# A 4 KB transfer of negated row maxima, issued by GpSimd instead of ScalarE

## The reference

```python
x = x + tanh(g_xattn[0]) * xattn(layernorm(x), ctx)      # fp8-rounded product, per batch 512 x 512
h = layernorm(x)
fused = h @ (Wa * col_scale)                             # queries, keys, values
scores = einsum('bhtd,bhsd->bhts', Qf, Kf) / sqrt(32)
scores = where(causal, scores, lowest)
attn = softmax(scores, axis=-1)                          # exp(s - max of the row) / sum
out = einsum('bhts,bhsd->bhtd', attn, V)
x = x + tanh(g_ffn[0]) * (out @ Wp)
```

## Time and profile before

| | us |
|---|---|
| median of 3 runs (lowest, highest) | 531.11 (529.98, 533.79) |
| profiled execution | 531.24 |
| its span, first to last instruction | 529.5 |
| TensorE busy | 458.1 (87%), mean granted clock 0.959 |
| VectorE busy | 336.6 (64%) |
| ScalarE busy, issues of transfers not counted | 272.3 (51%) |
| GpSimd busy | 144.5 (27%) |

### The profile page before, as it was taken

One profiled execution on the slowest core, in us unless ns is written; L12 is line 12 of the kernel. 1 busy time (PEld: TensorE's weight loads), 2 busy tenths in 40 slices (PEclk: granted clock), 3 DMA queues, 4 the chain that ended last, 5 costly groups with the idle time before them and its releaser, 6 DMA issues.

```text
span 529.5 us, 7878 instructions
## 1 busy us (share of the span) xinstructions
PE 458.1 (87%) x2536; PEld 325.8 (62%) x2536; DVE 336.6 (64%) x1110; ACT 272.3 (51%) x530; POOL 144.5 (27%) x264
## 2 busy tenths in 40 slices
PE   0477777998889999998779999998898999999994
PEld 0355556765555788765554878865564878676762
DVE  4997442698995244598996242677997244556634
ACT  2994326695545461595636452495655324444430
POOL 5849161252215200243214300233122100111210
PEclk9999997999878999999987999998989999999999
DMA  6411434323500245314400244314400143333002
GB/s 232 165 34 48 158 85 105 81 49 96 145 2 2 71 105 159 95 35 101 138 19 2 51 104 136 125 26 99 98 6 2 45 102 93 82 95 106 22 20 80
DMA packets 28025, 42.62 MB, mean 80 GB/s; under 512 B 8272, under 2 KB 8528, under 8 KB 27984
## 3 DMA queue, kind: packets, MB, share of 16 engines
q1 hardware_dynamic: 26448, 41.97, 28.5%
q10 hardware_dynamic: 1536, 0.14, 0.2%
HBM read 12.59 MB, written 4.19 MB: 32 GB/s over the span
## 4 chain that ended last, share of the span: by engine, by line
PE 58%; ACT 18%; DVE 13%; SPq 3%; issue 3%; DMA 2%; POOL 2%; ACTq 1%; DVEq 0%; POOLq 0%
PE pv_bank L716 11%; PE mm_bank L564 7%; PE mm_bank L565 6%; PE mm_bank L566 6%; PE exp_bank L702 5%; DVE x_all L1201 5%; PE max_bank L685 5%; ACT work L984 4%; DVE max_bank L1235 3%; SPq L374 3%; PE mm_bank L743 2%; PE mm_bank L744 2%; PE mm_bank L745 2%; PE turn_bank L580 2%; ACT tile_buf L931 2%
## 5 line engine op out<-in xcount | busy, mean ns | idle before, releaser
L1235 DVE CUSTOM_DVE_ANT_0 max_bank<-max_bank,causal 128x512 f32<-128x512 f32 (+3 forms) x256 | 119.2, 517 | 65.4 <-PE max_bank L685 65.0
L482 POOL TENSOR_SCALAR_AFFINE_SELECT work<-work 128x384 f32<-128x384 f32 x64 | 33.4, 521 | 299.4 <-ACT work L984 299.4
L984 ACT ACTIVATE work<-exp_bank 128x512 f32<-128x512 f32 (+1 forms) x192 | 90.9, 526 | 25.5 <-PE exp_bank L702 24.5
L716 PE MATMUL pv_bank<-work,v_aug 128*33 128x256 f32 (+3 forms) x512 | 83.6, 473 | 0.0
L702 PE MATMUL exp_bank<-q_stack,k_stack 97*128 97x512 f32 (+3 forms) x256 | 68.9, 353 | 4.1 <-ACT work L984 1.6
L685 PE MATMUL max_bank<-k_stack,q_stack 96*128 96x512 f32 (+3 forms) x256 | 61.7, 342 | 10.4 <-DVE row_max L1235 6.5
L716 PEld LDWEIGHTS pv_bank<-work,v_aug 128*33 128x33 f32 x512 | 29.0, 118 | 54.2 <-issue 48.5
L1218 DVE SCALAR_TENSOR_TENSOR qk_lo<-mm_bank,col_root,qk_hi 128x512 fp32r<-128x512 f32 x32 | 24.0, 750 | 59.2 <-ACT qk_hi L957 59.1
L1201 DVE SCALAR_TENSOR_TENSOR x_all<-mm_bank,coef,x_all 128x128 f32<-128x128 f32 x224 | 61.0, 342 | 0.8 <-PE mm_bank L612 0.8
L685 PEld LDWEIGHTS max_bank<-k_stack,q_stack 96*128 96x128 f32 x256 | 45.9, 196 | 17.8 <-issue 7.0
L702 PEld LDWEIGHTS exp_bank<-q_stack,k_stack 97*128 97x128 f32 x256 | 43.3, 188 | 19.7 <-ACT work L984 9.0
(11 more groups left out here) (161 smaller groups left out, 812.6 us busy)
## 6 DMA issues: line engine op xcount, KB each, us to landing
q_stack<-qk_hi SPq DMA_DIRECT2D x128, 64.0 KB, 2.0
k_stack<-qk_hi SPq DMA_DIRECT2D x128, 64.0 KB, 2.0
x_all<-in_x SPq DMA_DIRECT2D x16, 256.0 KB, 4.0
ctx_raw<-in_ctx SPq DMA_DIRECT2D x16, 256.0 KB, 4.4
q_stack<-qk_lo SPq DMA_DIRECT2D x64, 64.0 KB, 2.0
k_stack<-qk_lo SPq DMA_DIRECT2D x64, 64.0 KB, 2.0
out<-x_all SPq DMA_DIRECT2D x16, 256.0 KB, 2.3
work<-in_L_ffn_Wa SPq DMA_DIRECT2D x3, 768.0 KB, 9.7
```

Source lines behind the costliest of these rows:

```text
L482: pool.affine_select(out=three, in_=three, compare_op=ALU.is_ge, fill=0.0, base=0, pattern=[[0, 3], [1, P]], channel_multiplier=-1)
L716: last = pe.matmul(pv_bank[64 * j:64 * j + D + 1, P * m:T], v_aug[:, m, 2 * u + j, :], prob[j][:, PROB_COL[m]:PROB_COL[m] + T - P * m], st ...
L984: act.activation(prob[j][:, UNIT_COL[k]:UNIT_COL[k] + UNIT_LEN[k]], exp_bank[(3 * j + k) % 2][:, 0:UNIT_LEN[k]], ACT.Exp, scale=SCALE).the ...
L1235: last = dve.tensor_tensor_reduce(max_bank[unit % 2][:, col:col + width], max_bank[unit % 2][:, col:col + width], causal[:, T - width:T], ...
```

## The change

The transfer of the negated maxima into row 96 of `q_stack` leaves `negate_max` on ScalarE and becomes `place_max(b, u)` on GpSimd, at the head of each step, ahead of the pieces of gap 0. Source, destination, slot and semaphore remain. ScalarE's wait for its own negation moves with it, as GpSimd's wait. Because `neg_max` exists once and ScalarE no longer issues the transfer that reads it, ScalarE now waits, from the second step on, for the previous step's transfer to have landed before it negates again.

```diff
@@ gpsimd
+            def place_max(b, u):
+
+                s = u % SLOTS
+                pool.wait_ge(s_neg, 8 * b + u + 1)
+                pool.dma_start(q_stack[96:97, s, :, :].rearrange("p j (i t) -> p (j i) t", i=NT).bitcast(FP32),
+                               neg_max[:].bitcast(FP32)).then_inc(s_negrow[s], 16)
+
...
                 for u in range(STEPS):
+                    place_max(b, u)
                     fill(POOL_GAPS[u][0])
                     zero_future(b, u, 0)
...
@@ scalar
             def negate_max(n, u):
-                s = u % SLOTS
+                if u or n:
+                    act.wait_ge(s_negrow[(u - 1) % SLOTS], 16 * (2 * (n - (u == 0)) + (u - 1) % STEPS // SLOTS + 1))
                 act.wait_ge(s_mt, 8 * n + u + 1)
                 act.activation(neg_max[:], turned_max, ACT.Copy, scale=-1.0).then_inc(s_neg, 1)
-                act.wait_ge(s_neg, 8 * n + u + 1)
-                act.dma_start(q_stack[96:97, s, :, :].rearrange("p j (i t) -> p (j i) t", i=NT).bitcast(FP32),
-                              neg_max[:].bitcast(FP32)).then_inc(s_negrow[s], 16)
```

## The result

The changed kernel took 551.18 us (median of 4 runs, 545.36 to 554.72), the kernel before beside it 530.55. The ratio is 1.035, its 95% interval 1.023 to 1.047. Executions more than 1.5% above the fastest of their kernel count in the medians given here but not in the ratios, so 551.18 stands beside a ratio that is 549.0 over 530.55. A second series of the same kernel gave 548.23 us and 1.034 (1.026 to 1.042). The forecast was 555 with a range of 538 to 576 and the direction slower: both hold. By the ratio the change costs some 18 us (12 to 25) where the sum had 23.

A forecast was written before the change was run, and what follows sets the result against it. The prediction took TensorE's in-order instructions and waits as the bound, the transfer's 2.1 us cover being used up. Its terms, 5.6 + 3.4 + 5.5 + 7.4 - 1.2 + 2.6 = 23.3 us, gave 555 us, range 538 to 576.

The forecast's parts named there:

- (a): Last batch, eight steps, GpSimd free: rows land 0.8 us later each, less 0.8 us to spare together; +5.6 us.
- (d): Eighth step of the first two batches: transfer behind three scale-and-clip pairs, TensorE stands 3.8 and 3.6 us; +7.4 us.
- (f): TensorE's clock: falls after each of the two eighth-step waits, 1.3 us each; +2.6 us.
- (b): Nine steps of the first three batches, GpSimd free and the load close behind: late rows cost +3.4 us.
- (c): Third step of the first three batches: transfer stands behind two scale-and-clip pairs, three times 1.85 us; +5.5 us.
- ScalarE's relief: Rival: ScalarE, bound in second to fourth steps of three batches, gains nine times 0.65 us; 525 us, chance 0.03.
- (e): Fourth step of the first three batches: without ScalarE's issue TensorE's key product is there about 0.4 us sooner; -1.2 us.
- The cheap transfer: Rival: the transfer lands in 1.76 us from GpSimd too; 537 to 540 us, chance 0.17.
- The dear one: Rival: landing takes 3.2 us or more; about 575 us at 3.2, 595 us at 3.9; chance 0.12.
- Slack elsewhere: Rival: TensorE's mid-batch waits for VectorE's sums shrink by what it was late; 532 to 536 us, chance 0.06.

The follow-up runs named there:

- The repairs: Changed kernel with the transfer issued ahead of GpSimd's scale pairs in eighth steps and between them in third: 536.81 us, 1.015; eighth steps alone: 539.03 us, 1.018.

## Why the prediction held, step by step

**The sum.** Direction and range held, and the places of the loss were the right ones. The sizes were not: (a) to (d) were forecast at 21.9 us and measured 13.9, while the clock (f) cost 2.1 us more than forecast, so the total is nearer than its terms, and that is luck. By its own sign of being wrong, a landing not near 2.5 us, the prediction fails in that one term.

**The bound.** The central statement was that the cover of the transfer, the weighted values, is used up. It held: the row's lateness reached TensorE in the steps that had been just in time, and the chain of waits changed as it said, though with six of the last batch's eight transfers and not all eight. What I took for its proof was read wrongly: the twelve waits of 3.5 us in the earlier trace rows are for the most part the 0.20 us that stand there in any case; that the load followed the landing by 0.04 us in the earlier trace rows was the sound sign. And these steps, (a) and (b), are the smaller part of the cost, 4.5 us against 14.1 for (c), (d) and (f).

**Landing and hand-over.** This is the term that was mis-sized. I took 2.5 us for the landing and 0.05 for the hand-over; measured are 2.09 on average (median 1.9, 1.57 to 2.91) and a hand-over 0.26 longer than before, and ScalarE's landings in the trace of before were 1.90 on average, not the 1.76 of the best ones. So a row lands about 0.5 us later and not 0.8. I reasoned that GpSimd's issue would be the slower one from the length of its two-input instructions (1.04 us); its issue takes 0.52 to 0.65 us (0.78 once), and what is new is the hand-over, which I had priced from an engine that waits for itself. The two figures for the first byte in the Trainium skill, page "DMA: Bandwidth & Descriptors", section "Latency and other measured facts", had given an estimate of 2.16. The mean of 2.09 is nearer to that than to my 2.5, while the measured difference of the means, 0.18 us, is under half of the 0.4 between the Trainium skill's two figures, and the quickest landings go the other way (1.57 us from GpSimd, 1.75 from ScalarE).

**(a), (b)** came out at 3.5 and 1.0 instead of 5.6 and 3.4. In (a) it is that one error, and three stragglers (2.88, 2.47 and 2.32 us) carry 2.7 of the 3.5. In (b) it is that and another: the second steps' small net, which I put down to ScalarE's relief by the earlier trace rows, is slack, as the kernel with the added wait alone shows.

**(c), (d)** were right in place and mechanism, and too dear by the same landing: 1.84 and 1.76 us in the first of each. With these for 2.5 my own sums give 112.89 + 1.84 + 0.04 - 113.58 = 1.19 and 171.22 + 1.76 + 0.04 - 169.99 = 3.03, against 1.10 and 3.00 measured. The repairs show that both come from the pairs ahead of the issue.

**(e)** 1.0 for 1.2. **(f)** 4.7 for 2.6: the clock fell behind both waits of (d), as forecast, but stayed low into the query product and not only for as long as 16 matmuls of weighted values; a wait of 3 us cost 4.6 to 5.9. In the seventh step of the first batch, to which I gave no clock term, the weighted values take 4.1 us instead of 2.8 too, which is part of the rest in the table. Such stretches also move about without a cause that I could name, from 7 to 17 of them in the profiles of these kernels.

**ScalarE's wait** costs nothing that the times show, as said; in the traces it is 0.06 us a step.

**The rivals.** The cheap transfer (537 to 540) did not happen though the landings are mostly cheap: it had left out hand-over and stragglers, and had too little clock. The dear one is refuted by the landings. Slack elsewhere, as a rival for the whole, fell; in small it is there, in the second steps and in the third, of whose lateness 0.2 us is back by the next transposition in the first two batches. ScalarE's relief is real in the three fourth steps, 1 us in all.

## What to carry to other kernels

Before a small transfer is moved to an engine that looks idle, read three numbers in the trace: what runs on that engine at the very moment of the issue (its list, not its busy share: 27% busy, and yet 5.4 us late twice), how much work the consumer has between issue and need, and what a stall there does to TensorE's clock afterwards, which here cost nearly as much again as the stall. Put the issue ahead of the long instructions in the engine's list: here that took 3.4% down to 1.5%. If it is moved at all, then in the steps in which the old engine was behind; here that was worth at most 0.6%. And a wait of TensorE that was filled with other work saved nothing here, where the late data seems to head a chain through another engine.

## What the hardware showed that I had not expected

- **The hand-over to GpSimd takes 0.29 us**, ScalarE's to its own queue 0.03, with GpSimd idle for 1 to 2 us in both steps shown.
- **Landings from GpSimd fall in two groups.** Eleven of the 32 are issued with no issue of SyncE from 2 us ahead to 1.6 behind; six of them landed in 1.57 to 1.76 us and five in 2.47 to 2.90, in steps that look alike. The late ones are mostly the same steps: in the four profiles with all 32 transfers on GpSimd at the head of their steps the fifth of the first batch took 2.46 to 2.69 us, the first of the second batch 2.86 to 3.05, the seventh of the last 2.43 to 2.79. So it is something of the place, not chance; what, stays open. It need not be GpSimd: the fifth of the first batch lands late from ScalarE too (2.85 us in the kernel before, 2.56 to 2.90 in every kernel in which ScalarE issues it), while the first of the second batch (2.02) and the seventh of the last (1.81) do not.
- **Twice the packets.** The queues on the page, changed kernel (packets, MB, share):

```profile
q0 software_dynamic: 1024, 0.13, 0.2%
q10 hardware_dynamic: 1024, 0.01, 0.1%
```

and the same queue of ScalarE before:

```profile
q10 hardware_dynamic: 1536, 0.14, 0.2%
```

  32 transfers of 4 KB are 1024 packets from GpSimd, 32 for each, and were 512 from ScalarE, 16 for each. The Trainium skill, page "DMA: Bandwidth & Descriptors", section "Why a DMA increments its semaphore by 16 and not by 1", says that with the software generator all 16 engines report, whatever the shape, and with the hardware one only those that took part. The trace agrees: its records of the semaphore have 16 increments for each transfer of GpSimd's and 9 for each of ScalarE's, in the second step of the last batch one after 1.06 us, ahead of the first packet with data (1.27), and eight from 1.60 to 1.75. The packets of one transfer are 8 of 512 bytes and 24 of 4 bytes from GpSimd, and 8 and 8 from ScalarE.
- **The stragglers hang on single increments.** TensorE's load waits for the last of the 16. Of the ten landings over 2.3 us in the second series' profile, seven have fifteen increments within 2.1 us and the last one alone 0.6 to 1.2 us behind them. In the fifth step of the last batch the eight packets with the data start within 1.15 us of the issue, fifteen increments are there after 1.76 us, and the last one comes after 2.88. In the other three (2.87, 2.91 and 2.32 us) nine or all of the increments are late. Why one of them is late stays open.
- **One small transfer may delay another** of a different queue: by 0.6 us on average in the last batch of the kernel with the extra copy, in the one profile there is of it.
